# Twelve gather slots and twelve-step loop bodies in the attention loops of a GATv2 network

## The reference

```python
def gatv2_layer(x, Wl, bl, Wr, br, att, bias, src, dst, n):
    xl = (x @ Wl + bl).reshape(n, H, C)
    xr = (x @ Wr + br).reshape(n, H, C)
    e = leaky_relu(xl[src] + xr[dst], 0.2)
    logits = einsum('ehc,hc->eh', e, att)
    m = segment_max(logits, dst)
    p = exp(logits - m[dst])
    denom = segment_sum(p, dst)
    alpha = p / (denom[dst] + 1e-16)
    out = segment_sum(xl[src] * alpha[:, :, None], dst)
    return out.mean(axis=1) + bias
# three layers: x = batchnorm(leaky_relu(h, 0.01) + x), the last without the leaky_relu
# then x = layernorm(x + ...), and an equivariant network of one layer over the same edges
```

## Time and profile before

| what | before |
|---|---|
| median of 3 runs | 9731.46 us |
| lowest, highest run | 9714.06 us, 9761.34 us |
| span of the profiled execution | 9709.8 us |
| POOL, busy | 5006.8 us (52%) |
| gathers of the attention (line 488) | 2880 |
| copies of source numbers (line 480) | 480 |
| instruction queue 14 | 175 packets |

### The profile page before, as it was taken

The page is one execution under the profiler, slowest core; times in us unless marked ns, Lnnn a source line. Parts: engine busy times, 40 slices in busy tenths (PEclk is TensorE's granted clock), DMA queues, the critical chain, the costliest instruction groups (busy, mean ns, idle before and its releaser), DMA issues. The chain is left out here.

```text
span 9709.8 us, 177827 instructions
## 1 busy us (share of the span) xinstructions
PE 6604.5 (68%) x27124; PEld 4891.7 (50%) x27125; DVE 7234.8 (75%) x15343; ACT 3901.1 (40%) x14623; POOL 5006.8 (52%) x5548
## 2 busy tenths in 40 slices
PE   1677777775577777775577777775466666666666
PEld 0455555544355455544355555554455555555555
DVE  6577777673577677774567677775699999999999
ACT  0244444451144444442144444443144444444443
POOL 2554555421555455530445555540266666666666
PEclk7798899895789899986689889997555555555555
DMA  2111111110111111110111111120000000000000
GB/s 87 30 28 28 28 29 31 27 15 0 30 29 30 27 29 28 31 20 0 26 26 29 28 29 29 28 28 0 22 17 17 17 18 17 17 17 18 17 17 17
DMA packets 219588, 234.03 MB, mean 24 GB/s; under 512 B 74765, under 2 KB 200718, under 8 KB 219150
## 3 DMA queue, kind: packets, MB, share of 16 engines
q1 hardware_dynamic: 95630, 166.18, 5.7%
q0 software_dynamic: 123776, 66.31, 5.4%
HBM read 219.39 MB, written 12.80 MB: 24 GB/s over the span
## 5 line engine op out<-in xcount | busy, mean ns | idle before, releaser
L488 POOL DMA_INDIRECT xg<-table,idx x2880 | 2878.2, 999 | 1239.9 <-issue 818.4
L607 PE MATMUL psum<-wz,xt 128*128 x6072 | 2036.2, 430 | 572.6 <-ACT lin L803 426.7
L622 PE MATMUL psum<-px,oh 128*128 128x272 f32 x5760 | 1738.3, 427 | 379.4 <-issue 192.7
L607 PEld LDWEIGHTS psum<-wz,xt 128*128 128x128 f32 x6072 | 1013.9, 208 | 949.1 <-ACT xt L794 296.2
L622 PEld LDWEIGHTS psum<-px,oh 128*128 128x128 f32 x5760 | 1046.4, 202 | 881.6 <-issue 655.2
L1122 DVE SCALAR_TENSOR_TENSOR u<-psum,atts 128x512 f32<-128x512 f32 x1518 | 1039.9, 685 | 477.8 <-PE psum L609 229.0
L794 ACT COPY xt<-psum 128x256 f32<-128x256 f32 x1440 | 531.2, 369 | 1908.7 <-remote 819.8
L1149 DVE TENSOR_TENSOR px<-xs,pg 128x528 f32 (+1 forms) x1440 | 1010.0, 702 | 315.4 <-issue 238.0
L511 POOL DMA_INDIRECT xg<-table,idx x960 | 931.1, 970 | 582.7 <-issue 148.8
L738 PE MATMUL psum<-w2e,xt 65*128 65x256 f32 x1920 | 1087.0, 670 | 50.7 <-ACT xt L893 45.6
L746 PE MATMUL psum<-acc,oh 128*128 128x32 f32 x1920 | 509.3, 406 | 891.4 <-DVE acc L1480 889.2
(11 more groups left out here) (270 smaller groups left out, 10019.8 us busy)
## 6 DMA issues: line engine op xcount, KB each, us to landing
dr<-dlocs SPq DMA_DIRECT2D x480, 192.0 KB
xg<-table,idx POOLq DMA_INDIRECT x3840
acc<-w_rows SPq DMA_DIRECT2D x160, 192.0 KB
fl<-flags SPq DMA_DIRECT2D x30, 576.2 KB
flags<-fl SPq DMA_DIRECT2D x10, 576.2 KB, 3.2
table<-xn SPq DMA_DIRECT2D x4, 784.0 KB, 3.6
xp<-keys SPq DMA_DIRECT2D x5, 385.0 KB, 4.4
u<-keys SPq DMA_DIRECT2D x5, 385.0 KB, 4.4
```

What stands on the lines that cost most here:

```text
L488: nc.gpsimd.indirect_dma_start(out=xg[:, s, t, 96:128], out_offset=None, in_=table, in_offset=bass.IndirectOffsetOnAxis(ap=idx[:, s, t:t + ...
L607: pe.matmul(out_z, xt[:, r, e * P:(e + 1) * P], wz[:, bass.ds(l, 1), :].rearrange("p o z -> p (o z)"), start=True, stop=False)
L622: last = pe.matmul(agg_ps(r), oh[:, r, e, :], px[:, r, e, :], start=(e == 0), stop=(e == 1))
```

## The change

The body of the attention loops gets twelve steps (`SB` = 12), and a group four bodies. `xg`, `idx` and `dr` get twelve slots, there are twelve semaphores `gat` and four `drl`. POOL copies the source numbers of six steps with one instruction and waits for six `front`s before it. The counters that a slot's reuse waits for start at `FRONT0` = 16 instead of 8. To make room, `at` lies in `dr`, `dlb` in `xs`, and `w2e` in `acc`, at times when these are not in use. The unchanged functions that a body calls are not repeated here.

```diff
 S6 = 6
-BODIES = 8
-GS = S6 * BODIES
+SB = 12
+BODIES = 4
+GS = SB * BODIES
 AHEAD = 8
+FRONT0 = 16
...
-        idx = sb("idx", [P, S6, 2], I32)
-        xg = sb("xg", [P, S6, 2, P])
+        idx = sb("idx", [P, SB, 2], I32)
+        xg = sb("xg", [P, SB, 2, P])
-        dr = sb("dr", [P, S6, PAIR], BF16)
+        dr = sb("dr", [P, SB, PAIR], BF16)
...
-        gat = [sem(f"gat{s}") for s in range(S6)]
-        drl = [sem(f"drl{h}") for h in range(2)]
+        gat = [sem(f"gat{s}") for s in range(SB)]
+        drl = [sem(f"drl{h}") for h in range(4)]
...
             def load_places(l, g, i):
-                for half in range(2):
-                    n = steps_of(l, g, i, 3 * half)
-                    k0 = (g * BODIES + i) * S6 + 3 * half
-                    sp.wait_ge(oht_done, AHEAD + n - 3)
+                for part in range(4):
+                    n = steps_of(l, g, i, 3 * part)
+                    k0 = (g * BODIES + i) * SB + 3 * part
+                    sp.wait_ge(oht_done, FRONT0 + n + 3 - SB)
...
                     with pool.Fori(0, BODIES) as i:
                         body = (l * GROUPS + g) * BODIES + i
-                        k0 = (g * BODIES + i) * S6
+                        k0 = (g * BODIES + i) * SB
                         for half in range(2):
-                            a = 3 * half
-                            pool.wait_ge(front_done, AHEAD + l * ZS + k0 + a + 3 - S6)
-                            nc.gpsimd.tensor_copy(idx[:, a:a + 3, :], srci[:, bass.ds(k0 + a, 3), :]).then_inc(idx_done, 1)
+                            a = S6 * half
+                            pool.wait_ge(front_done, FRONT0 + l * ZS + k0 + a + S6 - SB)
+                            nc.gpsimd.tensor_copy(idx[:, a:a + S6, :], srci[:, bass.ds(k0 + a, S6), :]).then_inc(idx_done, 1)
                             pool.wait_ge(idx_done, AHEAD + 2 * body + half + 1)
-                            for s in range(a, a + 3):
-                                pool.wait_ge(front_done, AHEAD + l * ZS + k0 + s + 1 - S6)
-                                pool.wait_ge(xs_done, AHEAD + l * NS + k0 + s + 1 - S6)
+                            for s in range(a, a + S6):
+                                pool.wait_ge(front_done, FRONT0 + l * ZS + k0 + s + 1 - SB)
+                                pool.wait_ge(xs_done, FRONT0 + l * NS + k0 + s + 1 - SB)
...
             def pe_body(l, g, i, a, b, ends_group):
-                for s in range(S6):
-                    if a and (s + 2 < S6 or not ends_group):
-                        front(l, k0 + s + 2, (s + 2) % S6, t + (s + 2) // S6)
+                for s in range(SB):
+                    if a and (s + 2 < SB or not ends_group):
+                        front(l, k0 + s + 2, (s + 2) % SB, t + (s + 2) // SB)
```

More of the change, by code:

```diff
@@ L403, in load_places @@
             def load_places(l, g, i):
-                for half in range(2):
-                    n = steps_of(l, g, i, 3 * half)
-                    k0 = (g * BODIES + i) * S6 + 3 * half
-                    sp.wait_ge(oht_done, AHEAD + n - 3)
-                    sp.dma_start(dr[:, 3 * half:3 * half + 3, :].rearrange("p s e -> p (s e)"),
-                                 dlocs[0, bass.ds(k0 * PAIR, 3 * PAIR)].partition_broadcast(P)).then_inc(drl[half], 16)
+                for part in range(4):
+                    n = steps_of(l, g, i, 3 * part)
+                    k0 = (g * BODIES + i) * SB + 3 * part
+                    sp.wait_ge(oht_done, FRONT0 + n + 3 - SB)
+                    sp.dma_start(dr[:, 3 * part:3 * part + 3, :].rearrange("p s e -> p (s e)"),
+                                 dlocs[0, bass.ds(k0 * PAIR, 3 * PAIR)].partition_broadcast(P)).then_inc(drl[part], 16)
             with sp.Fori(0, LAYERS) as l:
@@ L625, in pe_body @@
             def pe_body(l, g, i, a, b, ends_group):
-                k0 = (g * BODIES + i) * S6
+                k0 = (g * BODIES + i) * SB
                 t = (l * GROUPS + g) * BODIES + i
-                for s in range(S6):
-                    if a and (s + 2 < S6 or not ends_group):
-                        front(l, k0 + s + 2, (s + 2) % S6, t + (s + 2) // S6)
-                    if a and (s + 1 < S6 or not ends_group):
+                for s in range(SB):
+                    if a and (s + 2 < SB or not ends_group):
+                        front(l, k0 + s + 2, (s + 2) % SB, t + (s + 2) // SB)
+                    if a and (s + 1 < SB or not ends_group):
                         zed(l, k0 + s + 1, (s + 1) % 2)
@@ L814, in act_body @@
                                 mg[:, 2 * j:2 * j + 2, bass.ds(c, 1), :].rearrange("p e o h -> p e (o h)")).then_inc(pm_done, 1)
-                    if a and (s + 2 < S6 or not ends_group):
+                    if a and (s + 2 < SB or not ends_group):
                         keep(l, g, i, k0 + s + 2, s + 2)
                     if a:
-                        linear(l, k0 + s, r, (g * BODIES + i) * 2 + s // J, s // J, s % J)
+                        linear(l, k0 + s, r, (g * BODIES + i) * (SB // J) + s // J, s // J % 2, s % J)
             def act_group(l, g, a, b):
@@ L1050, in _ @@
             op.tensor_scalar(valid, dl, 0.0, None, ALU.is_ge)
-            op.tensor_copy(dlb[:], dl)
+            op.tensor_copy(dlb, dl)
             seq(None)
@@ L1105, in _ @@
             op.tensor_scalar(real[:, BLOCKS - 1:BLOCKS], iota_p[:], float(N - (BLOCKS - 1) * P), None, ALU.is_lt)
-            for counter in (u_done, r_done, l_done, oht_done, px_done, acc_done, gb_done, h_done):
+            v.sem_inc(oht_done, FRONT0)
+            for counter in (u_done, r_done, l_done, px_done, acc_done, gb_done, h_done):
                 v.sem_inc(counter, AHEAD)
@@ L1139, in chunk_logits @@
             def chunk_logits(l, g, i, half):
-                n = ((g * BODIES + i) * 2 + half) * J + J - 1
-                logits(l, n, half, J, lg[:, :, bass.ds(i * 2 + half, 1), :].rearrange("p k o h -> p (k o) h"))
+                n = ((g * BODIES + i) * (SB // J) + half) * J + J - 1
+                logits(l, n, half % 2, J, lg[:, :, bass.ds(i * (SB // J) + half, 1), :].rearrange("p k o h -> p (k o) h"))
             def weigh_rows(l, g, i, k, s):
-                r, c, j = s % 2, i * 2 + s // J, s % J
+                r, c, j = s % 2, i * (SB // J) + s // J, s % J
                 m = l * NS + k
-                v.wait_ge(xs_done, AHEAD + m + 1)
+                v.wait_ge(xs_done, FRONT0 + m + 1)
                 v.wait_ge(agg_done, AHEAD + m - 1)
-                rows = xs[:, bass.ds((l * GROUPS + g) % 2, 1), bass.ds(i * S6 + s, 1), :, :].rearrange("p o q e c -> p (o q e) c")
+                rows = xs[:, bass.ds((l * GROUPS + g) % 2, 1), bass.ds(i * SB + s, 1), :, :].rearrange("p o q e c -> p (o q e) c")
                 op.tensor_tensor(
@@ L1167, in dve_body @@
                         weigh_rows(l, g - 1, i, k0 - GS + s, s)
-                    if a and s == J:
-                        chunk_logits(l, g, i, 0)
+                    if a and s % J == 0 and s > 0:
+                        chunk_logits(l, g, i, s // J - 1)
                     if a and s == 0 and not starts_group:
-                        chunk_logits(l, g, i - 1, 1)
-                    if a and (s + 3 < S6 or not ends_group):
+                        chunk_logits(l, g, i - 1, SB // J - 1)
+                    if a and (s + 3 < SB or not ends_group):
                         one_hot_t(l, g, i, k0 + s + 3, s + 3)
```

38 lines of the change are left out of this document (19 added, 19 removed).

## The result

| | before | after |
|---|---|---|
| median | 9722.76 us (4 runs) | 10,862.41 us (4 runs) |
| lowest to highest | 9698.36 to 9761.34 | 10,850.21 to 10,866.39 |
| span of the profiled execution | 9709.8 us | 10,859.6 us |

The changed kernel takes 1.117 times as long, 95% interval 1.1143 to 1.1197. The forecast of 9810 us and the range up to 10,150 were both missed.

What follows compares the result with a forecast made beforehand. PE waiting for gathered rows and POOL for slots, with PE's results late in long trains, was taken as the bound; +89 us (a and b) and -9 (a alone) gave 9790, plus 21.7 to the runs' median: 9810 us, range 9050 to 10,150.

Steps and rivals of the forecast that it cites:

- The third rival: Rival for POOL's gather trains: late results stay late until the train ends; cycle 25.0 us, time 10,560 us, chance 0.16.
- the second half: Last six gathers of a twelve-gather train (7.5 us): PE and DVE were to finish 1.55 steps there.
- The lower bound of 1.1: Fewest steps PE and DVE were to finish during the last six of twelve gathers; the upper bound was 2.0.
- the row with x2: Stretch of 10.3 us in the earlier trace, with no rest ahead, in which line 1122 ran twice.
- inside the steps as counted: PE's lower granted clock, 0.58 to 1.00 in three stretches, got no term of its own beside the counted steps.
- X: Cycle of six steps on POOL, from one copy of source numbers to the next: 21.3 us with a and b.
- The formula for a whole pass: Pass with a and b: six free steps and 7 cycles, 14.4 + 7 x 21.3 = 163.5 us, +3.3 us each.
- The passes with a alone: Three passes with a and without b: cycle of six steps 19.2 us, -9 us for the three together.
- The parts costed at nothing: Loads of `dr` further ahead, three moved buffers: no cost, at worst a few us once; doubled code left to a rival.
- The doubled code: Rival for DVE's and PE's doubled bodies: code no longer stays loaded, +133 us, time 9940 us, chance 0.04.
- The first rival: Rival for POOL's waits: twelve slots cover the late results; time 9060 us, or 8750 at a 16.0 us cycle; chance 0.20.

## Why the prediction was wrong

**The view of the bound was right, and the mechanism in its direction.** The reading of the earlier trace rows (what PE has finished reaches the others late in a long train, and they catch up when it ends) is what the increments show, and the change did make the loss grow with the train. The third rival, "nothing passes in a long train", had 0.16 and 10,560 us; 10,862 came out.

**The step that failed is "the second half"**, 1.55 steps as the middle between 1.1 and 2.0. It was zero: three `px` start in the train, the last at 730.88, and then none for 13.7 us. The lower bound of 1.1 came from the row with x2 in the earlier trace rows, where two trains of six have a pause of 1.23 us between them. I took that for twelve gathers in one train. It is two trains, and the steps counted in it may have come through around that pause; that they did is argued, not shown. A bound taken from the one pattern that still had a pause in it was no bound for a pattern with none.

**Two terms were left out.** The increments are not let go when the last gather ends but 2.1 us later, and the first step behind that runs at the lower clock, 4.6 us instead of 2.36; the prediction had what the clock costs "inside the steps as counted". With the first term alone, X = 16.0 + 2.1 + (6 - 2.2) x 2.36 = 27.1 us; measured, 27.3. That this fits is partly luck: three steps and not 2.2 have their `px` in the train, and the slow step behind it takes the difference. The rival's own 25.0 was short by these terms. The formula for a whole pass was too long in turn: with 27.3 it gives 7 x 27.3 + 14.4 = 205.5 us against 160.2, +45.3 us, where the pass grew by 36.5 in the first layer and by 40.8 and 40.4 in the others.

**A wait was read too long.** Of the 1.8 us that the prediction has POOL wait for a `front`, 1.36 are idle time ahead of the copy; the rest is one gather of 1.37 us instead of 0.95. That is 0.2 of a step.

**Why doubling the train more than doubles the loss.** Three steps lost 10.2 - 7.1 = 3.1 us before, six lose 27.3 - 14.2 = 13.1 now, against 6.2 for six before. An estimate of the hold, from about the third gather until the release: 4 x 1.25 + 1.1 = 6.1 us in a train of six, 10 x 1.25 + 2.1 = 14.6 us in one of twelve. So 3.0 us of work went on in the one and only 1.5 us net in the other. In the cycle above PE had finished what it could at 734.35, some 5 us into the hold; it then stood idle for 9.9 us and lost over 2 us more at the lower clock. How the 1150 us divide between waiting and clock was not measured; PE's 227.2 us more of busy time put the clock's part at up to a fifth, an estimate.

**The passes with a alone** came out at X = 22.6 us (copies at 301.11 and 323.75) where I had 19.2, for the same reason. The three passes grew by 96 us together, where -9 was forecast.

**The parts costed at nothing** held. `dr`: cutting its loads changes 0.3% late and 0.5% on time. The doubled code: queue 14 went from 175 to 415 packets, and they come spread over the time of the three layers (some 50 in 1000 us, where the kernel before had some 25), so code is indeed loaded anew in the loops. The changed kernel with these 415 packets is 5.9% faster than before where increments are on time. The Trainium skill ("Runtime: NRT & Kernel Launch", section "Instruction fetch mechanics") says that a taken branch to a target outside the two pages at hand forces a fetch; the packets agree with that, a price for it no run showed. `px` takes 700 ns in the changed kernel, and 708 without gathers: longer trains didn't slow it.

**The first rival** (latency was all) is what happens when increments are on time: copies 16.2 us apart against its 16.0, 8433 us against its 8750, of which some comes from a before that is itself 770 us shorter there. What the prediction couldn't know from one trace is that its central quantity isn't a constant of the kernel. That "slower" came true is in this respect luck: on time the same edit made the kernel 6% faster.

## What to carry to other kernels

A chain that hands results on by semaphores from PE beside long unbroken trains of indirect DMAs on POOL may run at two very different speeds, so a batch that is made longer "to save a pause" can put off the end of the train, at which the results come through. And an engine that stands idle that long can come back at a lower clock. Before lengthening such a train, look at the waiting engine's idle time behind a matmul that had long ended, and at where in the train it falls; and time the change in more than one sitting, since the same edit gave 0.94 and 1.12. Of the kernels tried, one copy a step won where increments are late (0.9255), six steps a copy where they are on time (0.9415, with three steps at 0.9447). Which of them is best over both kinds is not known: twelve slots with one copy a step ran only late, with three steps a copy only on time.

## What was unexpected

- Increments of PE, and of no other engine that could be read clearly, are held back (by a median of 11.8 us at the fourth of twelve gathers), and mostly let go together behind a train of gathers (1.13 us after one of six, 2.05 us after one of twelve, medians), in some sittings; in others at most 3% of the same program's come over 0.5 us late at any place of a train.
- The two kinds aren't told apart by the number of the chip (13 was both). Within a sitting all runs agree: in the last late one, seventeen runs of two kernels lay between 9683 and 9755 us.
- What holds the increments remains open. Excluded are the loads of `dr` (late, 1.0029) and the reloading of code (415 packets on time as well as late). Not told apart, since their runs all fell on on-time sittings, are density against rest, and PE's read of the block number.
